# Causal attention with q and k as two F32R words on the halves of the array, maxima over pairs of banks and exponentials over single banks

## What is computed

```python
xn = _layernorm(x)
q = (xn @ Wq.T).reshape(B, S, H, hd).transpose(0, 2, 1, 3)      # H = 16, hd = 16
k, v = ...                                                      # likewise
scores = einsum('bhcd,bhsd->bhcs', qi, k) * scale               # scale = 1/4
scores = where(kpos <= qpos, scores, min)
p = softmax(scores, axis=-1)
s = einsum('bhcs,bhsd->bhcd', p, v) ... @ Wo.T
x = x + s * silu(ffn(xn))                                       # a mixture of 8 experts
```

## Time and profile before

| | |
|---|---|
| device time, median of 3 runs | 2695.51 us (2693.76 to 2695.58) |
| span of the profiled execution | 2692.8 us |
| instructions | 51134 |
| busy in the span: TensorE, VectorE, ScalarE, GpSimd | 2451.3, 1846.2, 1406.8, 815.1 us |
| weight loads (overlapping matmuls) | 1589.0 us |

### The profile page before, as it was taken

How to read it: one execution, slowest core, us unless ns; L and a number is a source line. 1 busy time by engine, 2 the same in 40 slices (tenths; PEclk the granted TensorE clock), 3 DMA queues, 4 the chain that set the end, 5 groups by cost and what they waited for, 6 DMA issues and landing times. The chain is left out here.

```text
span 2692.8 us, 51134 instructions
## 1 busy us (share of the span) xinstructions
PE 2451.3 (91%) x16420; PEld 1589.0 (59%) x16420; DVE 1846.2 (69%) x3682; ACT 1406.8 (52%) x2776; POOL 815.1 (30%) x647
## 2 busy tenths in 40 slices
PE   5648999999999999969977599999999999999999
PEld 4512333333333333358866477777777777777777
DVE  7757877877787777424438476777667767766776
ACT  3404655656565566755634255555555555555554
POOL 1070000000000000014425355554455555444553
PEclk9858999999999999989988699999999999999999
DMA  4574041321404040033257000000000000000000
GB/s 135 191 170 65 5 62 26 41 52 16 61 6 62 6 60 5 7 127 133 102 177 241 18 13 12 11 13 13 13 13 13 9 11 13 13 13 13 13 9 9
DMA packets 189865, 132.85 MB, mean 49 GB/s; under 512 B 99857, under 2 KB 177687, under 8 KB 189712
## 3 DMA queue, kind: packets, MB, share of 16 engines
q1 hardware_dynamic: 160048, 100.06, 15.4%
q10 hardware_dynamic: 24160, 14.16, 2.2%
q0 software_dynamic: 5504, 16.69, 1.7%
HBM read 84.43 MB, written 46.14 MB: 48 GB/s over the span
## 5 line engine op out<-in xcount | busy, mean ns | idle before, releaser
L859 DVE TENSOR_REDUCE a_best<-a_ring 128x1 f32<-128x512 f32 (+3 forms) x1280 | 700.9, 604 | 214.0 <-PE a_ring L721 123.0
L836 ACT ACTIVATE a_probs<-a_pss 128x1024 f32<-128x1024 f32 (+3 forms) x640 | 554.0, 895 | 452.6 <-PE a_pss L777 228.7
L721 PE MATMUL a_ring<-a_kb,a_qa 96*128 96x512 bf16 (+3 forms) x1280 | 453.0, 365 | 67.2 <-DVE a_best L859 32.3
L774 PE MATMUL a_pss<-a_qa,a_kb 99*128 99x512 bf16 (+3 forms) x1280 | 433.9, 353 | 15.6 <-issue 7.2
L1771 ACT ACTIVATE w_probs<-w_pss,w_top 128x256 f32<-128x256 f32 x512 | 239.0, 476 | 379.7 <-DVE w_top L1859 365.0
L1606 POOL TENSOR_TENSOR w_probs<-w_probs,w_inv 128x512 f32<-128x512 f32 x256 | 301.0, 1176 | 395.7 <-DVE w_inv L1865 386.3
L962 POOL TENSOR_TENSOR e_w_r<-e_w,e_w_r 128x1024 fp32r<-128x1024 f32 x28 | 67.0, 2402 | 1032.7 <-ACT e_w_r L1035 1032.7
L1629 PE MATMUL w_psw<-wqkv,w_xr 128*128 128x512 f32 x1152 | 301.5, 398 | 11.6 <-POOL w_xr L1563 11.6
L774 PEld LDWEIGHTS a_pss<-a_qa,a_kb 99*128 99x128 bf16 x1280 | 123.5, 98 | 302.6 <-ACT a_probs L836 224.5
L792 PE MATMUL a_acc<-a_probs,a_vg 128*32 128x512 f32 (+3 forms) x2560 | 299.9, 541 | 0.1
L1669 PE MATMUL w_pss<-w_kd,w_qt 128*128 128x256 f32 x1536 | 278.4, 310 | 0.0
(11 more groups left out here) (223 smaller groups left out, 3771.2 us busy)
## 6 DMA issues: line engine op xcount, KB each, us to landing
e_w<-in_w SPq DMA_DIRECT2D x16, 1024.0 KB, 7.9
qk_parts<-p_parts SPq DMA_DIRECT2D x32, 384.0 KB, 3.7
a_qa<-qk_parts SPq DMA_DIRECT2D x192, 64.0 KB, 2.5
a_kb<-qk_parts SPq DMA_DIRECT2D x42, 256.0 KB, 9.5
p_xin<-in_x SPq DMA_DIRECT2D x8, 512.0 KB, 5.4
v_rows<-p_vout SPq DMA_DIRECT2D x8, 512.0 KB, 5.1
a_vg<-v_rows SPq DMA_DIRECT2D x32, 128.0 KB, 9.1
expert_in<-zero POOLq DMA_DIRECT2D x16, 256.0 KB, 8.3
```

The source lines that it names most:

```text
L721: ins = pe.matmul(bank[:, 0:keys], qa[u][0:QR, i // TC, h, (i % TC) * P:(i % TC + 1) * P], kb[u][0:QR, h, k * CH:k * CH + keys], start=Tru ...
L774: ins = pe.matmul(pss[idx % 2][:, e, lo:CH], kb[u][0:MR, h, j * P:(j + 1) * P], qa[u][0:MR, c, h, lo:CH], start=True, stop=(j < TC * c))
L836: act.activation(probs[:, idx % 4, :, lo:CH], pss[idx % 2][:, :, lo:CH], ACT.Exp).then_inc(exp_done, 1)
L859: vec.tensor_reduce(best[:, i // TC, h * TC + i % TC, k:k + 1], bank[:, 0:keys], X, ALU.max).then_inc(ring_taken, 1)
```

## The change

Projection cuts q and k into two F32R words instead of three bf16 ones; ScalarE makes the high word, VectorE the low one, straight from PSUM. In attention a head takes 48 rows (three combinations) and two more for the maximum, as two words. Heads go in pairs: one in rows 0 to 49 of the array, the other from row 64. An A step now covers both heads of a pair: two matmuls into a pair of banks, and one VectorE reduction over both; the ring has two pairs instead of three banks. An S step covers both heads too, in single banks, of which there are three; each has an exponential of its own. Masks are matmuls on halves of 64 rows: four for a pair of heads. The rows of ones in `kb` come by DMA from a new constant. The stores and loads have as many DMAs as before; those of the maximum have four a chunk instead of three. The constants gain sixteen steps for the masks on halves and one for the ones, and lose two.

```diff
-QR = 6 * HD
-MR = QR + 3
+QR = 3 * HD
+MR = QR + 2
+HALF = P // 2
@@ build_constants
+            for half, low_base in ((0, -HALF), (1, 0)):
+                for part, base in ((slice(0, P), low_base), (slice(0, HALF), HALF * half)):
+                    ch.link(pool.memset(keep["turn_halves"][part, half, :], 0.0))
+                    ch.link(pool.affine_select(out=keep["turn_halves"][part, half, :], ...))
+                    ch.link(pool.affine_select(out=keep["qk_halves"][part, half, :], ...))
+                    ch.link(pool.affine_select(out=keep["kq_halves"][part, half, :], ...))
+            ch.link(pool.memset(keep["ones32"][:, :], 1.0))
@@ stage_project
-        parts = st.sb("parts", [P, 4, 3, CH], BF16)
+        parts = st.sb("parts", [P, 4, 2, CH], F32R)
                 for m in range(4):
-                    rest_of(m)
-                for m in range(4):
-                    third(m)
+                    vec.wait_ge(high_part, 4 * c + m + 1)
+                    vec.scalar_tensor_tensor(out=parts[:, m, 1, :], in0=psq[m][:, :], ...
+                                             ).then_inc(parts_ready, 1)
-                for m in range(4):
-                    second(m)
-                    wait(pe, rest_ready, 4 * (c - 1) + m + 1)
+                    wait(pe, parts_ready, 4 * (c - 1) + m + 1)
@@ stage_attention
-RING = 3
+RING = 2
-        ring = [st.ps(f"ring{k}", [P, CH]) for k in range(RING)]
-        pss = [st.ps(f"pss{k}", [P, 2, CH]) for k in range(2)]
+        ring = [st.ps(f"ring{k}", [P, 2, CH]) for k in range(RING)]
+        pss = [st.ps(f"pss{k}", [P, CH]) for k in range(3)]
-            for u in range(2):
-                pool.memset(kb[u][QR:MR, :, :], 1.0).then_inc(ones_set, 1)
@@ a_step
+                for e in range(2):
+                    ins = pe.matmul(bank[:, e, 0:keys], qa[u][half(e, QR), i // TC, g, (i % TC) * P:(i % TC + 1) * P],
+                                    kb[u][half(e, QR), g, k * CH:k * CH + keys], start=True, stop=not diagonal)
                 if diagonal:
+                    for x in range(2):
+                        for e in range(2):
+                            ins = masked(bank[:, e, keys - P:keys], e, x, "qk_halves", x == 1)
@@ S
+                        pe.wait_ge(exp_done, primed + g * n_s + max(idx - 1, 0))
+                        for e in range(2):
+                            ins = pe.matmul(pss[(idx + e) % 3][:, lo:CH], kb[u][half(e, MR), hp, j * P:(j + 1) * P],
+                                            qa[u][half(e, MR), c, hp, lo:CH], start=True, stop=not diagonal)
+                            if not diagonal:
+                                ins.then_inc(s_ready, 1)
+                        if diagonal:
+                            for x in range(2):
+                                for e in range(2):
+                                    ins = masked(pss[(idx + e) % 3][:, lo:lo + P], e, x, "kq_halves", x == 1)
+                        idx += 2
@@ exponential
-                        act.activation(probs[:, idx % 4, :, lo:CH], pss[idx % 2][:, :, lo:CH], ACT.Exp).then_inc(exp_done, 1)
+                        for e in range(2):
+                            act.wait_ge(s_ready, g * n_s + idx + 1)
+                            act.activation(probs[:, (idx // 2) % 4, e, lo:CH], pss[idx % 3][:, lo:CH], ACT.Exp
+                                           ).then_inc(exp_done, 1)
@@ maximum
+                vec.tensor_reduce(best[:, i // TC, :, g * TC + i % TC, k], bank[:, :, 0:keys], X, ALU.max
```

More of the change, by code:

```diff
@@ L714, in _, with masked @@
         def _(pe):
+            def masked(bank, e, x, mask, stop):
+                return pe.matmul(bank, keep["turn_halves"][half(e, HALF), x, :], keep[mask][half(e, HALF), x, :],
+                                 start=False, stop=stop)
             def a_step(u, s, r, bank):
-                _, dg, h, i, k = s
+                _, dg, g, i, k = s
                 keys = min(CH, (i + 1) * P - k * CH)
```

193 lines of the change are left out of this document (96 added, 97 removed).

## The result

The changed kernel takes 2787.85 us (median; 2782.23 to 2798.05) where the kernel before, beside it on the same chip, takes 2695.55 (2693.76 to 2698.38): a ratio of 1.0336, 95% interval 1.0318 to 1.0354. That is 3.4% slower; forecast was 2678, range 2610 to 2765. The profiled execution's span is 2780.6 us against 2692.8, +87.8.

What follows compares the result with a forecast made beforehand. TensorE, busy 91% of the span, was taken as the bound. Constants +5.8, projection -10 and -2.5, head -12, seven groups -10, last group +12 gave -17 from 2692.8; with 2.7 for the median, 2678 us, range 2610 to 2765.

Steps and rivals of the forecast that it cites:

- A pair costs one slot: Attention's S and A matmuls: two heads on array halves take the time of one matmul, 0.22 us.
- Rivals 1 and 2: Attention's pairs: half loads run serially, 2743 us, chance 0.22; or halves do not overlap at all, 2819 us, chance 0.08.
- The loop of a full block, 2.90 us: Attention, PV to PV: second S waits for the same block's first exponential, so a block stays at 2.90 us.
- A-free block 2.68: Last attention group's blocks without A steps: need 2.68 us by the loop, where they took a mean of 2.08.
- Diagonal blocks: Attention's 16 masked blocks per group: masks and the wait in the loop add 4.3 us a group.
- Relief: Attention groups: of 16.2 us extra steps and ring waits, 5.7 go into the new wait; net -1.4 a group.
- The last group, +12: Last attention group: 20 blocks without A steps each take 0.6 us longer, +12 us.
- Constants +5.8 and projection -12.5: Before attention: uncovered POOL constant steps add 5.8 us; projection without third parts gains 10 us, and 2.5 after its last chunk.
- Head, -12: Start of attention: POOL's kb memsets go, so zeroing and scattering start sooner; -12 us, between -30 and +10.
- an earlier scatter ends that sooner: Start of attention: VectorE stood still 4.90 us at once while POOL scattered; scattering earlier would end this sooner.
- rival 3: Attention: TensorE's rests drop its clock to 1.2 GHz, five of 40 blocks at +1.55 us, +62, 2740 us; chance 0.10.

Runs made afterwards that it cites:

- e2: Changed kernel with every exponential cut to the first 128 columns of its score bank: 2675.35 us, one execution, against 2763.25 for the changed kernel on a like chip.
- e12: Changed kernel's data and packing with the old bank division (two pairs of score banks, ring of three single banks): 2786.74 us, ratio 1.0408 to the kernel before.
- e9: Changed kernel with the ring's four banks as four single ones, one maximum over 512 columns per head: 2773.56 us, ratio 1.0363 to the kernel before.
- e8: Changed kernel with at most one A step behind each S step, diagonal blocks weighed by their time: 2781.38 us, ratio 1.0437 to the kernel before.
- e10: Changed kernel with POOL zeroing and scattering only after K and Q have landed: 2750.30 us, ratio 1.0304 to the kernel before.
- e7: Changed kernel with POOL zeroing and scattering only after the first PV of attention: 2797.88 us against 2784.63 unaltered, ratio 1.035 to the kernel before.
- e4: Changed kernel with four single score banks and three single ring banks, A steps split by head: 2771.61 us, ratio 1.0357 to the kernel before.
- e6: Changed kernel with extra matmuls in the last group and A steps behind a block's first S computed twice: 2758.98 us against 2784.63 unaltered, ratio 1.0225.

## Why the prediction was wrong, and where it was right

Its own steps, in its order, with what the trace and the runs gave:

- **A pair costs one slot: right.** 0.33 us to the next pair behind a wait (0.10 + 0.22 said), 0.24 without one. The Trainium skill, "TensorE: Matmul & The Clock Gate", Part 3, says that matmuls in distinct row groups run concurrently; the trace agrees, two within 0.50 us. Rivals 1 and 2 are out: nothing is serial.
- **The loop of a full block, 2.90 us: right where it holds**, in ten of the 24 full stretches (nine of them 2.83 to 2.92 at full clock). **A-free block 2.68: right** (2.66 and 2.67 at full clock). e2 shows the exponential in the loop, e12 that the bank division put it there.
- **Diagonal blocks.** Forecast for the stretch with 256 columns 2.57 and for 128 2.09; measured 2.70 and 1.99 (before 2.22 and 1.63 at the same places, where the prediction had read 2.23 and 1.56). Where the four diagonal stretches of a chunk stand free of other changes they cost +1.3 and +1.6 us against the 1.07 summed for each. Right in kind, by these some 1 to 2 us a group too small; no run isolates them.
- **Relief: the step that failed in the loop.** It took 5.7 us off a group. The undisturbed group is +3.2 instead of -1.4, so diagonal blocks and relief together are off by 4.6 us, 32 us in seven groups, of which the diagonal blocks explain the smaller part. Some blocks did gain (3.91 to 2.85 at one place), but eleven of the 40 blocks have three A steps; between full blocks such a stretch takes 3.42 to 3.49 us instead of 2.85, for a ring of two pairs. The prediction named that ("three A in a block make TensorE wait") and gave it no price of its own. e2 shows that the exponential does not close these stretches, the trace after has TensorE wait for VectorE in them, and e9, with a finer ring, shortens them. But neither the order of e8 nor the single ring banks of e9 made the kernel clearly faster.
- **The last group, +12.** At full clock +15 (89.7 to 104.8, with repeats in it): nearly right. At the clock it was granted, +34.
- **Constants +5.8 and projection -12.5: right** (+5.9 and -12.3).
- **Head, -12: wrong**, +3.8. POOL issued its zeros 4.5 us after the start of attention instead of 18, but then waited for them twice as long (below; before 9.98). That goes with the loads of K and Q: issued when these have landed, the zeros are waited for 7.2 us (e10) and 7.5 us (e7). The first scatter came 33.8 us after the start of attention instead of 36.7. The step counted the start of the zeroing and not its end; and even these 2.9 us did not shorten the head, so that "an earlier scatter ends that sooner" failed too, for a reason that stays open. e10 ran on a chip without stalls and leaves untested whether waiting would help on the other kind.

```profile
130.95 8.75 POOL L652 DMA_DIRECT2D expert_in<-zero  x16 [0.32 <-POOL a_vg L647]
160.26 1.04 POOL L655 DMA_INDIRECT expert_in<-xn_all,slot_put  x1 [20.56 <-DMA expert_in<-zero]
```

- **The clock, the term that the sum put at nothing: the largest step that failed.** It stood only as rival 3, was given 0.10, and happened. It had been priced at five of 40 blocks, all groups alike. Its price of a block was right (1.55; the A-free block is 4.13 instead of 2.66, +1.47). The extent was not: it takes 19 us in the last group alone, and about 3.9 us net in each of seven others, some 46 us in all. The granted clock by pieces of 4 us, at the start of the second group in the trace after:

```profile
348.00:352.00 4.00, 2.63 (x26) 1.61 (x26) 2.54 (x4) 1.56 (x3) 0.00 (x0) 1.00 0.50 122
352.00:356.00 4.00, 3.56 (x26) 1.42 (x24) 2.69 (x3) 2.77 (x6) 0.00 (x0) 0.59 0.61 144
356.00:360.00 4.00, 4.00 (x34) 1.58 (x26) 1.39 (x2) 1.37 (x5) 0.00 (x0) 0.50 0.54 138
...
372.00:376.00 4.00, 3.91 (x28) 1.63 (x26) 2.42 (x4) 2.17 (x4) 0.00 (x0) 0.85 1.07 79
376.00:380.00 4.00, 3.15 (x26) 1.09 (x22) 3.08 (x3) 3.15 (x6) 0.00 (x0) 1.00 1.08 118
```

TensorE goes into this with some rest, is at 1.2 GHz for about 20 us, and comes out. At half clock it looks fully busy, so its busy share doesn't show the loss; the clock column does. The waits of the five groups answer to the loop: TensorE's weight loads for S waited 367 times for ScalarE, 250.2 us, where before it was 183 times and 138.9.

```profile
PEld a_pss L775 <- ACT a_probs L841: 250.2, 367, 1.7
```

```profile
PEld a_pss L774 <- ACT a_probs L836: 138.9, 183, 0.8
```

That these rests bring the clock down is shown by what filling them does, in the last group in five traces of five. For the other groups the amount of some 27 us is worked out from the shortest stretches and not isolated by a run; that the lost time lies in stretches at half clock is read from the trace.

The sum as it should have been: +5.9 - 12.3 + 3.8 (head) + 3.2 x 7 (groups, undisturbed) + 15 (last group) + 46 (clock) = +81, of 87.8 measured. The forecast had -17. Of the 98 us between the two sums the clock makes 46, relief with the diagonal blocks 32, the head 16 and the last group's loop 3. What decided the result was that the saved work turned into rest, and rest has a price of its own.

## What to carry to other kernels

When a change removes TensorE work inside a loop that something else then closes, count what TensorE's rest does to its clock as a term of the sum, not as a rival: here it was about half the loss. One block read well gives the loop of such blocks only: shortening the suspected link (e2) showed that more than half of the full stretches waited for something else. Before dividing PSUM banks anew, write down for each step which earlier one it waits for: one bank less between producer and consumer moved a wait from the block before to the same block, and the two other divisions of the eight banks that freed it (e4, e12) moved it to the ring. An undisturbed group, put together from the shortest occurrence of each stretch, tells structure from clock.

## What the runs showed of the hardware

- The granted clock of the same kernel on the same chip varied from 0.904 to 0.925 between executions, and the time by 40 us with it; the kernel before, at 0.950 to 0.953, varied by 9 us.
- Extra matmuls whose results are thrown away made the kernel faster: 2758.98 against 2784.63 us (e6).
- Zeroing 4 MB of device memory in 16 DMAs ended 20.4 to 20.6 us after the last was issued when K and Q were being loaded beside it, and 7.2 or 7.5 us after it when they were not (e10, e7).
- F32R weight loads of two halves, 48 or 50 rows, took 0.19 us together (183 ns each, so they overlap), where one bf16 load of 99 rows took 0.10; the first line is of the trace after, the second of the one before. A pair of 512-column matmuls followed another without a wait after 0.24 us (e12: 1200.72 and 1200.96 us).

```profile
1158.34 0.19 PEld L775 LDWEIGHTS a_pss<-a_qa,a_kb 50*128 50x128 f32 x2 [0.84 <-ACT a_probs L841]
```

```profile
602.42 0.10 PEld L774 LDWEIGHTS a_pss<-a_qa,a_kb 99*128 99x128 bf16 x1 [0.84 <-ACT a_probs L836]
```

```profile
1200.72 0.40 PE L722 MATMUL a_ring<-a_kb,a_qa 48*128 48x512 f32 x2
...
1200.96 0.40 PE L775 MATMUL a_pss<-a_qa,a_kb 50*128 50x512 f32 x2
```

- Chips differ in more than speed: the stretch from the start of attention to the first exponential is 97 us on one kind and 69 on the other, with the same code, and the 27 us follow POOL's zeroing and scattering when these are moved (e7).
